# The end of a fused cross-attention and feed-forward kernel, in another order

## The reference, cut to what matters

```python
x = x + xattn(layernorm(x), ctx)                 # ... the attention part
def ffn(x, ...):                                 # called as x + ffn(layernorm(x))
    thought = layer_norm(x)[:, -1, :] @ agg_w + agg_b      # one row per batch
    for _ in range(4):
        t = gelu(layer_norm(thought) @ d1_w + d1_b)
        thought = thought + (t @ d2_w + d2_b)
    broadcast = (thought @ bc_w + bc_b)[:, None, :]
    gate = sigmoid(x @ gate_w + gate_b)
    out = x + gate * broadcast
    return layer_norm(out) * out_gamma + out_beta
```

## Time and profile before

| what | us |
|---|---|
| median of 3 runs | 587.45 (586.84 to 589.7) |
| the profiled execution's own time | 589.54 |
| its span, first to last instruction | 587.7 |
| busy TensorE matmul / VectorE / ScalarE / GpSimd | 528.0 / 377.0 / 305.3 / 238.4 |
| mean granted TensorE clock | 0.954 of full |

### The profile page before, as it was taken

The page is one execution under the profiler, slowest core; times in us unless marked ns, Lnnn a source line. Parts: engine busy times, 40 slices in busy tenths (PEclk is TensorE's granted clock), DMA queues, the critical chain, the costliest instruction groups (busy, mean ns, idle before and its releaser), DMA issues.

```text
span 587.7 us, 9896 instructions
## 1 busy us (share of the span) xinstructions
PE 528.0 (90%) x3800; PEld 322.5 (55%) x3800; DVE 377.0 (64%) x773; ACT 305.3 (52%) x543; POOL 238.4 (41%) x142
## 2 busy tenths in 40 slices
PE   4999999697998999999999978898999989999860
PEld 3888878475754555465655544354445445554330
DVE  3488577397665666666675794466655737257766
ACT  4963467141464566266664642546543454685441
POOL 1320133020167355636663360334233526387343
PEclk9999999799998999999999988799999989799976
DMA  8975489547989687576776744242515413200001
GB/s 304 401 245 199 164 203 261 176 160 279 229 259 249 182 212 206 117 202 182 205 185 170 202 113 125 56 99 78 131 43 150 99 37 113 72 1 36 20 36 54
DMA packets 61327, 91.92 MB, mean 156 GB/s; under 512 B 4512, under 2 KB 29104, under 8 KB 60704
## 3 DMA queue, kind: packets, MB, share of 16 engines
q1 hardware_dynamic: 56848, 74.68, 45.5%
q0 software_dynamic: 3312, 14.51, 7.5%
q10 hardware_dynamic: 1120, 2.10, 1.1%
HBM read 71.87 MB, written 19.66 MB: 156 GB/s over the span
## 4 chain that ended last, share of the span: by engine, by line
PE 67%; DVE 13%; DMA 10%; ACT 5%; issue 3%; SPq 1%; POOLq 0%; POOL 0%; DVEq 0%; ACTq 0%
PE psum L734 12%; PE psum L843 11%; PE psum L807 10%; PE psum L824 10%; PE psum L848 5%; PE psum L880 5%; PE psum L969 3%; DMA qscr<-hl 3%; PE psum L934 3%; PE psum L915 2%; DMA in_wki<-wki 2%; DMA qst<-qscr 2%; DVE negt L1237 2%; PE psum L869 1%; DMA chx<-x2s 1%
## 5 line engine op out<-in xcount | busy, mean ns | idle before, releaser
L1071 ACT ACTIVATE prob<-psum 128x512 f32<-128x512 f32 x256 | 138.7, 594 | 132.1 <-PE psum L824 130.1
L1237 DVE TENSOR_REDUCE negt<-psum 128x1 f32<-128x512 f32 (+1 forms) x256 | 134.7, 547 | 60.7 <-PE psum L807 60.6
L1466 POOL TENSOR_TENSOR added<-added,prob 128x1024 f32<-128x1024 f32 x48 | 113.7, 2369 | 19.8 <-ACT prob L1071 14.8
L807 PE MATMUL psum<-kst,qst 96*128 96x512 f32 x256 | 98.1, 460 | 13.2 <-DVE negt L1237 9.1
L1463 POOL TENSOR_TENSOR added<-prob 128x1024 f32<-128x1024 f32 x16 | 38.1, 2384 | 159.1 <-ACT prob L1071 159.1
L824 PE MATMUL psum<-qst,kst 112*128 112x256 f32 x512 | 94.5, 304 | 2.3 <-ACT prob L1071 1.9
L824 PEld LDWEIGHTS psum<-qst,kst 112*128 112x128 f32 x512 | 80.0, 196 | 26.5 <-ACT prob L1071 12.3
L843 PE MATMUL psum<-prob,vring 128*32 128x256 f32 x1152 | 94.0, 411 | 0.0
L807 PEld LDWEIGHTS psum<-kst,qst 96*128 96x128 f32 x256 | 40.6, 191 | 71.6 <-issue 45.1
L1235 DVE TENSOR_REDUCE negt<-psum 128x1 f32<-128x257 f32 x128 | 53.1, 415 | 22.1 <-PE psum L807 21.9
L1416 POOL TENSOR_TENSOR ssum<-sq 128x512 f32<-128x512 f32 x6 | 8.6, 1440 | 80.1 <-ACT sq L1036 63.2
(11 more groups left out here) (157 smaller groups left out, 709.4 us busy)
## 6 DMA issues: line engine op xcount, KB each, us to landing
kst<-kscr SPq DMA_DIRECT2D x96, 256.0 KB, 5.7
vring<-vscr SPq DMA_DIRECT2D x16, 576.0 KB, 6.3
kscr<-hl SPq DMA_DIRECT2D x16, 512.0 KB, 2.8
d<-d POOLq DMA_DIRECT2D x8, 1024.0 KB, 6.9
qst<-qscr SPq DMA_DIRECT2D x48, 128.0 KB, 4.8
vscr<-vbuf SPq DMA_DIRECT2D x18, 256.0 KB, 2.9
qscr<-hl SPq DMA_DIRECT2D x8, 512.0 KB, 4.9
in_c<-ctxT SPq DMA_DIRECT2D x2, 1024.0 KB, 12.8
```

The lines of the kernel that those rows point to most:

```text
L807: pe.matmul(psum[:, n % 3, :], qst[0:96, slot, jj, qt * P:(qt + 1) * P], kst[0:96, slot, jj, half * 512:(half + 1) * 512], start=True, sto ...
L1071: act.activation(prob[:, r % NP, part], score2[:, part], ACT.Exp).then_inc(exp2_done, 1)
L1237: dve.tensor_reduce(negt[:, u % 2, qt, half, HPG + j:HPG + j + 1], psum[:, n % 3, k0:512], AX.X, ALU.max, negate=True)\
L1466: pool.tensor_tensor(added[:, :], added[:, :], prob[:, r % NP, :], ALU.add).then_inc(added_done, 1)
```

## The change

The plan's loops now stop at the end of the units (only steps before 128 are taken from them, for tiles 0 to 3, and `o(3, n)` is no longer placed by them), and the rest is a list written out by hand, in another order. Tiles 6 and 7 are normalised by VectorE (`x_norm`), each after its own rstd (`x_stat`); GpSimd's part of `x_norm` is the addition of beta. The mix of tile 7 is made by VectorE (`f_mix`). `f_out` has two passes instead of three, and the first does not wait for the rstd. The statistics in `o` use a buffer per tile. Semaphore `x2n_last` counts the two tiles that VectorE normalises.

```diff
-    for f in range(8):
-        if f >= 6:
-            s = max(s, 8 * NU + 2)
+    for f in range(4):
...
+            if s + n >= 8 * NU:
+                continue
...
-    for k in range(4):
+    for k in range(3):
...
-        if r % 8 == 1 and 8 < r <= 8 * NU + 1:
+        if r % 8 == 1 and 8 < r < 8 * NU:
             add('weigh', r // 8 - 1)
...
+    plan += [('f_gate', 3, 0), ('f_sig', 2), ('weigh', NU - 1), ('f_out', 1), ('f_norm', 4), ('f_gate', 3, 1), ('f_norm', 5),
+             ('f_exp', 3), ('f_sig', 3), ('f_stat2', 2),
+             ('o', 3, 0), ('f_turn', 4), ('x_stat', 6), ('f_out', 2), ('x_norm', 6),
+             ('o', 3, 1), ('f_turn', 5), ('x_stat', 7), ('f_stat2', 3), ('x_norm', 7),
+             ('f_gate', 4, 0), ('f_gate', 4, 1), ('f_out', 3), ('f_turn', 6), ('f_exp', 4), ('f_sig', 4),
+             ('f_gate', 5, 0), ('f_gate', 5, 1), ('f_turn', 7), ('f_exp', 5), ('f_sig', 5), ('f_stat2', 4), ('f_out', 4),
+             ('f_gate', 6, 0), ('f_gate', 6, 1), ('f_exp', 6), ('f_sig', 6), ('f_stat2', 5),
+             ('f_gate', 7, 0), ('f_gate', 7, 1), ('f_out', 5), ('f_exp', 7), ('f_sig', 7), ('f_stat2', 6), ('f_mix',),
+             ('f_stat2', 7), ('f_out', 6), ('f_out', 7)]
... ScalarE
+            def x_stat(f):
+                act.wait_ge(x2_stats, f + 1)
+                rstd(xterms[:, 0, f:f + 1], mv[:, f, 1:2], epsln[:, 0:1]).then_inc(x2_rstd, 1)
... VectorE
-                stats(residual(f), fst[:, f % 2, :], mv[:, f, :]).then_inc(x2_stats, 1)
+                stats(residual(f), bst[:, f, :], mv[:, f, :]).then_inc(x2_stats, 1)
...
+            def x_norm(f):
+                dve.wait_ge(x2_rstd, f - XS + 2)
+                dve.wait_ge(mix_done, f - NX + 1)
+                dve.tensor_scalar(x2n[:, f % NX, :], residual(f), mv[:, f, 0:1], xterms[:, 0, f:f + 1], ALU.subtract, ALU.mult)\
+                   .then_inc(x2n_last, 1)
+
+            def f_mix():
...
+                dve.wait_ge(gate_done, f + 1)
+                dve.wait_ge(*x2n_of(f))
+                link(dve.tensor_tensor(z, z, bcb1[:, :], ALU.mult))
+                link(dve.tensor_tensor(z, z, x2n[:, f % NX, :], ALU.add))
...
             def f_out(f):
                 z = zt[:, f % NX, :]
+                dve.wait_ge(f_stats, f + 1)
+                link(dve.scalar_tensor_tensor(z, z, fmv[:, f % 2, 0:1], rows[:, R_OG, :], ALU.subtract, ALU.mult))
                 dve.wait_ge(f_rstd, f + 1)
                 dve.wait_ge(x2b_ready, f + 1)
-                link(dve.tensor_scalar(z, z, fmv[:, f % 2, 0:1], frs[:, f % 2:f % 2 + 1], ALU.subtract, ALU.mult))
-                link(dve.tensor_tensor(z, z, rows[:, R_OG, :], ALU.mult))
-                dve.tensor_tensor(residual(f), z, residual(f), ALU.add).then_inc(out_ready, 1)
+                dve.scalar_tensor_tensor(residual(f), z, frs[:, f % 2:f % 2 + 1], residual(f), ALU.mult, ALU.add).then_inc(out_ready, 1)
... GpSimd
             def f_sig(f):
+                if f == 7:
+                    return
```

More of the change, by code:

```diff
@@ L51 @@
 F_EVERY = 3
-F_TAIL = 3
 LEAD = 4
@@ L229, in make_plan @@
     at(s, 'res2')
-    for f in range(8):
-        if f >= 6:
-            s = max(s, 8 * NU + 2)
+    for f in range(4):
         while (s + 4 + ahead) % 8 == 1 and s + 4 < 8 * NU:
             s += 1
-        if f in (0, XS):
-            at(s, 'f_terms', f // XS)
+        if f == 0:
+            at(s, 'f_terms')
         for n, e in ((1, ('f_norm', f)), (2, ('f_turn', f)), (3, ('f_gate', f, 0)),
@@ L240, in make_plan @@
                      (5, ('f_exp', f)), (6, ('f_sig', f)), (8, ('f_stat2', f)), (9, ('f_out', f))):
+            if s + n >= 8 * NU:
+                continue
             older = extra.setdefault(s + n, [])
             older.insert(1 if e == ('f_gate', f, 1) and older[:1] == [('f_gate', f, 0)] else 0, e)
-        s += F_EVERY if s < 8 * NU else F_TAIL
+        s += F_EVERY
     cut = {s for s, es in extra.items() for e in es if e[0] in ('ch_d1', 'ch_d2', 'f_gate') and e[2] > 0
            and not any(x[:2] == e[:2] and x[2] == 0 for x in es)}
-    for k in range(4):
+    for k in range(3):
         s = 8 * NG * (k + 1) + 2
@@ L251, in make_plan @@
                 s += 1
[L252 to L255, removed]
+            extra.setdefault(s, []).insert(0, ('o', k, n))
+            s += 1
+    assert max(extra) < 8 * NU
+    for r in range(8 * NU + 2):
         if r < 8 * NU:
@@ L287, in make_plan @@
         plan += post.get(r, [])
+    plan += [('f_gate', 3, 0), ('f_sig', 2), ('weigh', NU - 1), ('f_out', 1), ('f_norm', 4), ('f_gate', 3, 1), ('f_norm', 5),
[7 more added lines that the diff above has]
+             ('f_stat2', 7), ('f_out', 6), ('f_out', 7)]
+    assert len(plan) == len(set(plan))
     return plan
@@ L510, in build @@
         x2_terms = sem("x2_terms")
-        x2n_done = sem("x2n_done")
+        x2n_done, x2n_last = sem("x2n_done"), sem("x2n_last")
         z_ready = sem("z_ready")
@@ L559, in ctx_of, with x2n_of @@
             return T['ctxT'].rearrange("(k p) n -> p k n", p=P)[:, :, c0:c0 + 512]
+        def x2n_of(f):
+            return (x2n_done, f + 1) if f < XS else (x2n_last, f - XS + 1)
         block = ctx.enter_context(nc.Block())
@@ L955, in f_turn @@
                 ps = open_bank(job_at[('f_turn', f)])
-                pe.wait_ge(x2n_done, f + 1)
+                pe.wait_ge(*x2n_of(f))
                 for kc in range(KC):
@@ L1103, in ch_gelu, with f_terms @@
                 act.preload_act_table_set("natural_log_exp_and_others")
[L1105 to L1108, removed]
+            def f_terms():
+                act.wait_ge(x2_stats, XS)
+                rstd(xterms[:, 0, 0:XS], mv[:, 0:XS, 1], epsln[:, 0:1]).then_inc(x2_rstd, 1)
+            def x_stat(f):
+                act.wait_ge(x2_stats, f + 1)
+                rstd(xterms[:, 0, f:f + 1], mv[:, f, 1:2], epsln[:, 0:1]).then_inc(x2_rstd, 1)
             def f_norm(f):
-                act.wait_ge(x2_terms, 1 + f // XS)
+                act.wait_ge(x2_terms, 1)
                 if f >= NX:
@@ L1140, in _ @@
                      'S2': S2, 'ch_rstd': ch_rstd_of, 'ch_gelu': ch_gelu, 'f_terms': f_terms, 'f_norm': f_norm, 'f_turn': f_turn,
-                     'f_exp': f_exp, 'f_sig': f_sig, 'f_stat2': f_stat2,
+                     'f_exp': f_exp, 'f_sig': f_sig, 'f_stat2': f_stat2, 'x_stat': x_stat,
                      'shift': shift, 'spread': spread}
@@ L1355, in ch_spread, with f_terms @@
                 dve.tensor_copy((bcb0, bcb1)[b][:, :], psum[:, bank_of[job], :]).then_inc(emptied_by['dve'], 1)
-            def f_terms(i):
-                tiles = slice(0, XS) if i == 0 else slice(XS, 8)
-                dve.wait_ge(x2_rstd, i + 1)
+            def f_terms():
+                tiles = slice(0, XS)
+                dve.wait_ge(x2_rstd, 1)
                 dve.scalar_tensor_tensor(xterms[:, 1, tiles], mv[:, tiles, 0], -1.0, xterms[:, 0, tiles], ALU.mult, ALU.mult).then_inc(x2_terms, 1)
@@ L1373, in f_gate @@
                 dve.tensor_scalar(z, z, -41.0, None, ALU.max).then_inc(z_ready, 1)
+            def x_norm(f):
[4 more added lines that the diff above has]
+            def f_mix():
+                f = 7
+                z = zt[:, f % NX, :]
+                dve.wait_ge(gate_done, f + 1)
+                dve.wait_ge(*x2n_of(f))
+                link(dve.tensor_tensor(z, z, bcb1[:, :], ALU.mult))
+                link(dve.tensor_tensor(z, z, x2n[:, f % NX, :], ALU.add))
             def f_stat2(f):
-                dve.wait_ge(mix_done, f + 1)
+                if f < 7:
+                    dve.wait_ge(mix_done, f + 1)
                 stats(zt[:, f % NX, :], fst[:, f % 2, :], fmv[:, f % 2, :]).then_inc(f_stats, 1)
@@ L1390, in _ @@
                      'ch_spread': ch_spread, 'f_terms': f_terms, 'f_gate': f_gate,
-                     'f_stat2': f_stat2, 'f_out': f_out}
+                     'f_stat2': f_stat2, 'f_out': f_out, 'x_norm': x_norm, 'f_mix': f_mix}
             for e in plan:
@@ L1499, in f_norm @@
             def f_norm(f):
-                pool.wait_ge(x2n_done, f + 1)
+                pool.wait_ge(*x2n_of(f))
                 pool.tensor_tensor(residual(f), residual(f), rows[:, R_OB, :], ALU.add).then_inc(x2b_ready, 1)
             def f_sig(f):
+                if f == 7:
+                    return
                 h, b, _ = unit(NG * (f // 2))
@@ L1512, in _ @@
             steps = {'sumsq': sumsq, 'late': late, 'bias': bias, 'ch_hT': ch_hT, 'ch_sum': ch_sum, 'res2': res2, 'ch_d1': ch_d1, 'ch_ln': ch_ln, 'o': o, 'PV': PV, 'f_norm': f_norm,
-                     'f_sig': f_sig}
+                     'f_sig': f_sig, 'x_norm': f_norm}
             for e in plan:
```

## The result

| | before | after |
|---|---|---|
| median (runs) | 587.14 (586.56 to 589.7, 4) | 579.33 (576.36 to 580.81, 4) |
| ratio of the runs, 95% interval | | 0.9852 (0.9803 to 0.9901) |
| profiled execution, its span | 589.54, 587.7 | 576.36, 574.6 |
| tail: gate 3's first matmul to VectorE's last pass | 49.44 | 39.50 |

Run once more, the changed kernel had 577.35 (574.5 to 579.51, 6 runs), ratio 0.9831 (0.9785 to 0.9877). A ratio leaves out executions that are over 1.5% above the fastest of their kernel. Forecast: 579.2, 8.24 less. The profiled spans differ by 13.1, but only 9.94 of it lies in the tail, which is all that the change touches but for `f_out(0)`; the other 3.2 had come about before gate 3, see the first experiment. From here on the tail is the measure: times of runs scatter by several us, while the tail was 39.50 and, in the one repeat, 39.47.

A forecast was written before the change was run, and what follows sets the result against it. A chain between engines, none full, bounded the 46.60 us tail. Stepped through, VectorE needs 38.69 us (27.9 passes, 8.5 port waits, 2.3 idle), ending 8.24 earlier: 587.45 - 8.24 = 579.2 us, range 576.0 to 583.6.

The forecast's parts named there:

- the stepping: Hand walk through the tail, each instruction starting when engine and inputs are ready: 38.69 us on VectorE, ending at 577.05.
- rival A: Tail: VectorE is the bound and its port with GpSimd charges about ten turns; 579.2 us, chance 0.62.
- part 3: Port shared by VectorE and GpSimd: a met GpSimd pass costs VectorE up to 1.27 us; 8.5 in ten meetings.
- Part 2: Two-pass finishing in `f_out`: 0.44 us a tile, 3.1 for seven tiles, and the rstd wait of about 0.6 hidden.
- Part 1: Attention weighting moved ahead of `f_out(1)`, so that `o(3,0)` starts earlier: 0.33 us gained.
- Part 4: New order: norms 6 and 7 and mix 7 on VectorE, rstd per tile; TensorE nowhere idle over 0.4 us.
- The passes: VectorE's own instructions in the tail, without port waits and idles: 27.9 us of the 38.69.
- `f_out(0)`, taken as nothing: The one edit inside attention, its first pass going ahead of a GpSimd add: bounds -0.3 to +0.7 us, nothing counted.
- Rival B: Tail: new passes hardly wait at the port, gate 7 on TensorE sets the end; 576.4 us, floor 573.2, chance 0.14.
- C: Tail: more port turns, 16.5 us instead of 8.5, and idles; 583.7 us, 587 at the worst, chance 0.15.
- D: Norms 6 and 7 late, TensorE idles 4 us before their turns, gates 5 to 7 at 1.2 GHz; 591.7 us, chance 0.03.
- E: Tail: something unseen, such as a late mix, holds the same chain; within 0.5%, 586 us, chance 0.06.

The follow-up runs named there:

- the first experiment: The changed kernel run again unchanged: tail 39.47 us, ratio 0.9831 (0.9785 to 0.9877); unit 0 to unit 1 of the attention took 20.9 us.

## Why the prediction was right, step by step

Times from gate 3's first matmul, us; predicted ones from the stepping, measured ones from the changed kernel's trace:

| end of | predicted | measured |
|---|---|---|
| (start of) `o(3,0)` | 3.87 | 3.73 |
| `f_out(1)` | 7.3 | 6.0 |
| statistics of `o(3,0)` | 11.1 | 9.7 |
| norm 6 | 14.9 | 13.5 |
| `f_out(3)` | 20.8 | 19.3 |
| gate 5's clamp | 22.9 | 21.5 |
| gate 7 on TensorE | 26.8 | 26.4 |
| `f_out(4)` | 28.5 | 27.0 |
| `f_out(5)` | 33.8 | 32.3 |
| last pass | 41.2 | 39.5 |

- **The bound (rival A).** Right. A chain through all engines became VectorE's queue, busy but for two idles, at just the two places (mix 4, mix 6) and of the size (1.16 and 1.15 for 1.16 and 1.13) that the stepping gave.
- **The port (part 3), the term with the largest error.** 7.6 us in nine meetings for 8.5 in ten. Two meetings failed to come and one came that I did not have. I had GpSimd's mix 2 start ahead of `f_out(1)`, and it came 0.05 behind it; its 1.09 makes most of the 1.36 that the table shows at `f_out(1)`. The first pass of `f_out(2)` was not held (0.77 in the stepping), norm 6 was (1.48 for 0.53). These two cancel, by luck, and so the offset stays within 0.4 to the end. Each met finishing pass cost nearly what line 1219 had shown: 1.64 to 1.77 for 1.78. The Trainium skill's GPSIMD Engine Reference, Specifications, names VectorE instructions with two SBUF inputs or in a 2-port mode. The traces agree on the first: finishing passes were held, those with one input in PSUM not. Norm 6 and three clamps (up to 1.53 for 0.43) were held with one SBUF input, while the statistics, with one as well, were not (0.66 to 0.69); whether a 2-port mode makes that difference no run here shows. With GpSimd's passes cut none was held.
- **Part 2.** Sized at 3.1 in passes plus hidden waits; undone it costs 5.04, within the 4.3 to 6.5 of its expectation.
- **Part 1** came (0.14 more than said), but the two passes alone bring `o(3,0)` as early; it is not a gain of its own.
- **Part 4** was right in where TensorE stands (0.4 off at gate 7), and the cover that I gave it, 3.5, was 2.5. Not asked in the prediction: whether the two norms should be on VectorE (1.21 lost) and whether gate 6 should stand behind `f_out(4)` (1.80 lost). How much of the order's gain is TensorE's clock was not separated.
- **The passes** summed to 27.3 and not 27.9; back-to-back starts overlap a little more than I took off.
- **`f_out(0)`**, taken as nothing: the last unit of the attention, in which it lies, took 23.0 to 23.2 us in the three traces with three passes and 22.9 to 23.1 in the nine with two.
- Rival B's floor (35.2 in these terms) is close to the 35.0 that GpSimd's cut passes show. C is out by the port waits (7.6, where it had up to 16.5), D by TensorE (no idle, clock 1.00), E by the tail's 9.94.
- The total of 8.24 stood against 9.94 in the tail. Of the 1.70 between them, 0.9 are the port, 0.6 the passes and 0.15 the weighting. That the median difference of 7.8 comes so close to 8.24 is luck: it carries the scatter of the attention part, and the repeat has 10.1.

## What to carry to other kernels

Step the end of a program through by hand, engine by engine, with durations from the trace; where no engine is full, that found the next bound and its two idles here, and the total to 1.7 us. Which passes meet on VectorE and GpSimd is the part that a step of 0.05 us can turn. A pass off VectorE's queue is worth its time and its meetings less what VectorE then waits for: the shorter finishing gave more than its own time (5.04 for 3.1), the norms less (1.21 for 2.01), the mix less than nothing (-0.30). Then ask of each idle in the stepped list what else was ready: that gate 6's result would lie there while VectorE made `f_out(4)` stands in the stepping.

## What the runs showed of the hardware that was not expected

- TensorE's clock fell to the lower level without a long idle. With `f_terms` early the longest gap ahead of the slow gate was 1.04 us, TensorE busy for 11.78 of the 13.80 us before, and the gate took 5.37. The gaps came close together, though: between the end of gate 4 (547.69) and gate 5 (550.12) TensorE had only the four transposes of turn 5, 0.63 us. The stretches before and of that gate:

```profile
535.50:549.30 13.80, 11.78 (x32) 5.31 (x32) 7.84 (x15) 4.33 (x10) 4.83 (x4) 1.00 0.05 16
549.30:556.00 6.70, 5.86 (x13) 2.53 (x12) 5.96 (x9) 3.60 (x8) 5.10 (x4) 0.75 0.10 39
```

- A pass of two columns is held at the port too. The 1.22 us of `f_terms` in the kernel before, which the prediction calls "mostly waiting", are such a meeting: the pass ends 0.01 behind GpSimd's.

```profile
558.73 1.59 POOL L1510 TENSOR_TENSOR zt<-zt,x2n 128x512 f32<-128x512 f32 x1
559.12 1.21 DVE L1360 SCALAR_TENSOR_TENSOR xterms<-mv,xterms 128x2 f32<-128x2 f32 x1
```

- One stretch far ahead of the change took from 17.9 to 25.1 us in different executions, a spread of more than any part tested. TensorE's wait for a transfer in it, 0.4 to 3.6, goes with it but is at most half of the spread. What decides it is open.
